# Gathered rows turned by transposing DMAs from ScalarE instead of TensorE transposes and a copy: a routed feed-forward kernel on one Trainium2 core

## The chip, the cores and the metric

The kernel runs on one core of a Trainium2 chip. The metric is device time in microseconds, the median of three runs.

## The reference, cut to what matters

For each of four batches of 1024 tokens by 1024 features, a 0/1 mask `m` of the same shape is made first (the 10,240 largest entries of `softmax(x) * side * cond`, without the diagonal). The mask's rows are then the input of a mixture of eight experts, two chosen for each row, and the result is added to `x`:

```python
scores = softmax(m @ G); value, indices = top_k(scores, 2)
w      = one_hot(indices, 8) weighted with value          # [b, s, e]
gate   = silu(einsum('bsh,efh->bsef', m, gate_w))
up     = einsum('bsh,efh->bsef', m, up_w)                 # F = 128
out    = einsum('bsef,bse,ehf->bsh', gate * up, w, down_w)
lr     = einsum('bsh,erh->bser', m, lora_A)               # R = 16
out    = out + einsum('bser,bse,ehr->bsh', lr, w, lora_B)
result = x + out
```

## The kernel before, in words

All weights are cut into f16 parts and held in SBUF for the whole run. Each batch is worked off in `T` = 23 tiles of up to 128 (row, expert) pairs, each tile for one expert. The work is written out by hand for each engine's queue; every queue runs in order, and engines wait for each other on semaphores. `tile(n, i)` = 23 n + i numbers the tiles through all batches.

For tile i of batch n, in the order of the data:

- GpSimd (`gather`, L514) fetches the tile's rows of the mask from `mask_rows` in HBM by an indirect DMA into `xg`, a ring of `NX` = 3 buffers of 128 rows by 1024 f16. It waits until the rows of three tiles back have been turned. GpSimd's loop over i issues `gather(i + 3)`, then `put_out(i - 3)`, then work for the next batch's mask, then `sum_piece` of the batch before.
- TensorE (`turn_x`, L668) transposes the tile's eight 128x128 blocks into one PSUM bank, and ScalarE (`store_xt`, L840) copies the bank to `xt`, two buffers of eight blocks. The copy waits until the first layer of two tiles back has read the buffer (`l1_done`).
- TensorE (`first_layer`, L681) multiplies: 16 matmuls with the blocks of `xt` as weights and `w1` moving, into `pa`.
- ScalarE (`silu`, L845) and VectorE (`gate`, L1342 to L1350) make the gated product; TensorE (`turn_g`, L692) transposes it, VectorE stores it, and TensorE (`second_layer`, L704 to L707) makes 2 x 4 matmuls of 512 columns into `pc`.
- ScalarE (`store_y`, L853) scales into `y`, and GpSimd (`put_out`, L522) scatters the rows to `put_rows` in HBM by an indirect DMA.

TensorE's queue for step i is: `first_layer(i)`, `turn_x(i + 2)`, `turn_g(i - 1)`, `second_layer(i - 2)`, with pieces of the next batch's work between them. ScalarE's is: `silu(i)`, `store_xt(i + 2)`, both halves of `store_y(i - 2)`, with counts of the next batch's mask (tiles 3 to 6, 8 and 9) and copies of its transposed mask (tiles 18 to 22) between them. A batch starts with `turn_x` of tiles 0 and 1.

Beside this, the results of the batch before are put together in 16 pieces of 128x512 (one per step in steps 1 to 9 and 13 to 19), in two buffers `piece`: SyncE loads x and the two scattered rows of each token (L367, L369), GpSimd adds them (L531, L534), SyncE stores the sum (L376) and only then loads the next piece into that buffer. Near the end of batches 0 to 2 SyncE (`move_mask`) loads the x of the batch after next, or for the last time the x of the last batch, and stores the finished mask to `mask_rows`. After the last batch SyncE loads the scattered rows, VectorE adds (L1449) and SyncE stores.

Of the kernel before, what the change touches and what calls it, by code (L numbers as in the profile page):

```python
# [6 lines left out]
ACT = mybir.ActivationFunctionType  # L7
AX = mybir.AxisListType
F32 = mybir.dt.float32
F16 = mybir.dt.float16  # L10
BF16 = mybir.dt.bfloat16
I32 = mybir.dt.int32
U32 = mybir.dt.uint32

P = 128
# [18 lines left out]
def build(nc, x, side, cond, G, gate_w, up_w, down_w, lora_A, lora_B, out):  # L34
# [70 lines left out]
    with ExitStack() as ctx:  # L105
# [6 lines left out]
        def sem(name):  # L112
            return ctx.enter_context(nc.semaphore(name))
# [121 lines left out]
        def table_of(n, i, dt=F32):  # L235
# [17 lines left out]
        l1 = [pa[:, i, 0:N1] for i in range(2)]  # L253
        xt_ps = blocks(pb[:, 0, :])
        gt_ps = blocks(pb[:, 1, :])[:, 0:3, :]
        mt_ps = blocks(pd[:, :])

        xt_words, gt_words, mt_words = pb[:, 0, :], pb[:, 1, 0:3 * P // 2].bitcast(I32), pd[:, :]
        words_of = lambda a, dt: a.rearrange("p t k -> p (t k)").bitcast(dt)
# [44 lines left out]
        last_summed, last_stored = sem("last_summed"), sem("last_stored")  # L304
        xt_turned, xt_ready, l1_done, silu_done = (
            sem(n) for n in ("xt_turned", "xt_ready", "l1_done", "silu_done"))
        g_ready, gt_turned, gt_ready, y_done, y_ready = (
# [14 lines left out]
        def tile(n, i):  # L322
            return T * n + i
# [4 lines left out]
        def _(sp):  # L328
# [50 lines left out]
            def move_mask(n):  # L379

                sp.wait_ge(mask_ready, n + 1)
                if n + 1 < B:
                    load_side(n + 1)
                    load_x(n + 1)
                else:
                    for c in range(C):
                        sp.dma_start(v[:, c, :], x_rows[n][:, c, :]).then_inc(last_x_landed[c], 16)
                if n >= 2:

                    sp.wait_ge(xt_turned, tile(n - 1, 0))  # L390
                sp.dma_start(mask_rows[n % 2].rearrange("(p c) h -> p (c h)", c=C),
                             mask[:, :]).then_inc(mask_stored, 16)
# [39 lines left out]
        def _(pool):  # L432
# [77 lines left out]
            def gather(n, i):  # L510
                g = tile(n, i)
                if g >= NX:
                    pool.wait_ge(xt_turned, g - NX + 1)
                pool.indirect_dma_start(  # L514
# [46 lines left out]
        def _(pe):  # L561
# [99 lines left out]

            def turn_x(n, i):
                g = tile(n, i)
                pe.wait_ge(gathered[g % NX], 16 * (g // NX + 1))
                if g > 0:
                    pe.wait_ge(xt_ready, g)
                for t in range(HT):
                    last = pe.transpose(xt_ps[:, t, :], xg[:, g % NX, t * P:(t + 1) * P], ident[:, :])  # L668
                last.then_inc(xt_turned, 1)

            def load_expert(n, i):
                return pe.value_load(expert[n][0:1, i:i + 1], min_val=0, max_val=E - 1)

            def first_layer(n, i, e):
                g = tile(n, i)
                pe.wait_ge(xt_ready, g + 1)
                if g >= 2:
# [56 lines left out]
            for n in range(B):  # L734
                pe.wait_ge(routed, n + 1)
                turn_x(n, 0)
                turn_x(n, 1)
                experts = {}
# [21 lines left out]
                for i in range(T):  # L760
                    experts[i] = load_expert(n, i)
                    first_layer(n, i, experts[i])
                    between(i, 0)
                    if i + 2 < T:
                        turn_x(n, i + 2)
                    between(i, 1)
# [17 lines left out]
        def _(act):  # L784
# [49 lines left out]

            def store_xt(n, i):
                g = tile(n, i)
                act.wait_ge(xt_turned, g + 1)
                if g >= 2:
                    act.wait_ge(l1_done, g - 1)
                nc.scalar.activation(words_of(xt[:, g % 2, :, :], F32), xt_words, ACT.Copy).then_inc(xt_ready, 1)  # L840

# [55 lines left out]
            for n in range(B):  # L897
# [8 lines left out]

                store_xt(n, 0)
                store_xt(n, 1)
                for i in range(T):
                    silu(n, i)  # L910
                    between(i, 0)
                    if i + 2 < T:
                        store_xt(n, i + 2)
                    between(i, 1)
# [565 lines left out]
```

## Time and profile before

| | |
|---|---|
| time, median of 3 runs | 810.81 us (809.69 to 813.43) |
| the profiled execution's own time | 809.9 us |
| its span, first to last instruction | 808.2 us |
| TensorE matmuls (PE), busy | 518.8 us (64%) |
| VectorE (DVE), busy | 515.5 us (64%) |
| ScalarE (ACT), busy | 403.3 us (50%) |
| GpSimd (POOL), busy | 391.1 us (48%) |
| mean granted clock of TensorE | 0.846 |

Times in the views count from the start of the span. PEld is the loading of weights, which runs beside the matmuls; SPq, POOLq and DVEq are an engine's own queue. Busy shares are means over stages with different limits: the first 160 us make the first mask and cut the weights, then come four batches of 23 tiles, and from about 770 us on the last batch's results are put together. Of an arrow `a<-b`, a is written and b read; buffer numbers are left out. An arrow behind a wait names what ended it.

### The profile page before, as it was taken

The page shows a single profiled execution, that of the slowest core. Times are in us where ns is not written, and L with a number is a line of the kernel's source. Part 1 is how long each engine was busy: PE and PEld are TensorE (multiplying, and loading weights), DVE is VectorE, ACT ScalarE, POOL GpSimd, SP SyncE. Part 2 cuts the span into 40 slices and gives each one's busy share as a digit, 9 for nine tenths or more (in the row PEclk, how much of TensorE's full clock was granted, in tenths as well). Part 3 has the DMA queues.
Part 4 walks back from the last instruction along what each step waited for, and adds up shares of the span by engine and source line. Part 5 has one row for each costly group of instructions (what it writes and reads, how often), then busy time and mean ns, then how long its engine had stood idle before and what let it go on. Part 6 is the DMA issues. An engine that isn't in the chain of part 4 may idle for free.

```text
span 808.2 us, 14610 instructions
## 1 busy us (share of the span) xinstructions
PE 518.8 (64%) x4178; PEld 356.4 (44%) x4178; DVE 515.5 (64%) x1242; ACT 403.3 (50%) x655; POOL 391.1 (48%) x337
## 2 busy tenths in 40 slices
PE   0211287179878964778787917787798288897900
PEld 0200276056645633455455515554556155565500
DVE  5768889766798575865884776747872623233335
ACT  5687277739734463376344453783344234354400
POOL 8114200125484114477886125878872167767510
PEclk9755599579999895899999868998989779899965
DMA  9990160024323734478377834685579258868469
GB/s 313 360 264 0 51 263 27 13 65 157 121 105 113 276 126 130 150 250 283 133 258 256 340 101 157 218 293 186 192 247 380 81 153 291 270 215 271 173 253 381
DMA packets 80443, 159.93 MB, mean 198 GB/s; under 512 B 22889, under 2 KB 32105, under 8 KB 79856
## 3 DMA queue, kind: packets, MB, share of 16 engines
q1 hardware_dynamic: 59760, 108.60, 39.4%
q0 software_dynamic: 20608, 50.37, 17.9%
q8 instruction: 43, 0.70, 0.4%
q14 instruction: 32, 0.26, 0.1%
HBM read 107.53 MB, written 73.40 MB: 224 GB/s over the span
## 4 chain that ended last, share of the span: by engine, by line
DMA 26%; POOL 18%; issue 16%; DVE 14%; PE 13%; ACT 6%; DVEq 3%; SPq 3%; POOLq 1%; ACTq 0%
DMA out_dram<-piece 7%; DMA piece<-put_rows 7%; DMA put_rows<-y,where 6%; POOL piece L531 4%; DMA xg<-mask_rows,where 4%; POOL piece L534 4%; PE pa L681 4%; POOL xg L514 3%; ACT mask L796 3%; POOL put_rows L522 3%; DVE w L1172 2%; DMA w<-put_rows 2%; DVE mask L1066 2%; PE pb L668 2%; ACT y L853 2%
## 5 line engine op out<-in xcount | busy, mean ns | idle before, releaser
L681 PE MATMUL pa<-w,xt 128*128 x1472 | 199.4, 289 | 1.2 <-issue 1.2
L853 ACT ACTIVATE y<-pc,where 128x512 f32<-128x512 f32 x184 | 124.5, 686 | 105.9 <-PE pc L707 82.2
L681 PEld LDWEIGHTS pa<-w,xt 128*128 128x128 f16 x1472 | 147.0, 100 | 56.6 <-issue 10.5
L514 POOL DMA_INDIRECT xg<-mask_rows,where x92 | 100.0, 1087 | 122.9 <-DVEq L1334 94.8
L522 POOL DMA_INDIRECT put_rows<-y,where x92 | 92.2, 1003 | 130.9 <-ACT y L853 109.8
L1342 DVE SCALAR_TENSOR_TENSOR g_full<-pa,where,s_act 128x144 f32<-128x144 f32 x92 | 33.6, 365 | 180.4 <-ACT s_act L845 180.0
L668 PE MATMUL pb<-ident,xg 128*128 128x128 f16 x736 | 62.8, 234 | 77.1 <-DMA xg<-mask_rows,where 58.1
L840 ACT ACTIVATE xt<-pb 128x512 f32<-128x512 f32 x92 | 55.0, 598 | 109.1 <-PE pb L668 105.5
L668 PEld LDWEIGHTS pb<-ident,xg 128*128 128x128 f16 x736 | 49.7, 105 | 87.7 <-DMA xg<-mask_rows,where 61.6
L845 ACT ACTIVATE s_act<-pa,small 128x128 f32<-128x128 f32 x92 | 33.8, 367 | 98.3 <-PE pa L681 98.3
L704 PE MATMUL pc<-wd,gt 128*128 x184 | 75.7, 411 | 5.4 <-ACT y L853 5.3
L705 PE MATMUL pc<-wd,gt 128*128 x184 | 75.3, 409 | 0.0
L531 POOL TENSOR_TENSOR piece<-piece 128x512 f32<-128x512 f32 x48 | 61.1, 1272 | 28.5 <-DMA piece<-put_rows 28.0
L706 PE MATMUL pc<-wd,gt 128*128 x184 | 74.7, 406 | 0.0
L707 PE MATMUL pc<-lb,gt 128*128 x184 | 74.4, 405 | 0.0
L796 ACT ACTIVATE mask<-v,small 128x1280 f16<-128x1280 f32 x48 | 65.0, 1355 | 8.2 <-POOL v L470 5.5
L534 POOL TENSOR_TENSOR piece<-piece 128x512 f32<-128x512 f32 x48 | 62.7, 1307 | 3.8
L1350 DVE TENSOR_TENSOR g_parts<-g_full,g_parts 128x144 f16<-128x144 f32 x92 | 44.7, 486 | 6.8
L937 DVE TENSOR_REDUCE small<-v 128x1 f32<-128x1024 f32 x32 | 38.4, 1214 | 14.9 <-DMA v<-in_x_dram 14.6
L1010 DVE TENSOR_SCALAR_CACHE_REDUCE mask<-v,small 128x1024 f16<-128x1024 f32 x36 | 44.9, 1273 | 2.8 <-POOL v L470 2.1
L957 DVE SCALAR_TENSOR_TENSOR v<-v,small,t_row 128x1024 f32<-128x1024 f32 x32 | 43.6, 1400 | 0.7
L692 PE MATMUL pb<-ident,g_parts 128*128 128x128 f16 x276 | 32.4, 229 | 15.0 <-DVE gt L1358 14.9
(208 smaller groups left out, 864.0 us busy)
## 6 DMA issues: line engine op xcount, KB each, us to landing
piece<-put_rows SPq DMA_DIRECT2D x96, 256.0 KB
v<-in_x_dram SPq DMA_DIRECT2D x40, 512.0 KB, 8.9
piece<-in_x_dram SPq DMA_DIRECT2D x48, 256.0 KB
out_dram<-piece SPq DMA_DIRECT2D x48, 256.0 KB
mask_rows<-mask SPq DMA_DIRECT2D x4, 2048.0 KB, 17.5
w<-put_rows SPq DMA_DIRECT2D x16, 512.0 KB, 9.9
w<-in_L_ffn_gate_w_dram SPq DMA_DIRECT2D x8, 512.0 KB, 10.2
w<-in_L_ffn_up_w_dram SPq DMA_DIRECT2D x8, 512.0 KB, 8.3
```

The source lines that it names most:

```text
L514: pool.indirect_dma_start(out=xg[:, g % NX, :], out_offset=None, in_=mask_rows[n % 2], in_offset=bass.IndirectOffsetOnAxis(ap=mask_row[n][ ...
L522: pool.indirect_dma_start(out=put_rows[n % 2], out_offset=bass.IndirectOffsetOnAxis(ap=put_row[n][:, i:i + 1], axis=0), in_=y[:, g % NY, : ...
L531: nc.gpsimd.tensor_tensor(piece[:, at, 0, :], piece[:, at, 0, :], piece[:, at, 1, :], ALU.add).then_inc(half_summed, 1)
L534: nc.gpsimd.tensor_tensor(piece[:, at, 0, :], piece[:, at, 0, :], piece[:, at, 2, :], ALU.add).then_inc(summed_piece, 1)
L668: last = pe.transpose(xt_ps[:, t, :], xg[:, g % NX, t * P:(t + 1) * P], ident[:, :])
L681: last = pe.matmul(l1[g % 2], xt[:, g % 2, t, :], w1[:, bass.ds(e, 1), t, k, :].rearrange("p o n -> p (o n)"), start=(t == 0 and k == 0), ...
L704: pe.matmul(pc[:, half, :], high, own(wd[:, bass.ds(e, 1), 0, cols]), start=True, stop=False)
L705: pe.matmul(pc[:, half, :], high, own(wd[:, bass.ds(e, 1), 1, cols]), start=False, stop=False)
L706: pe.matmul(pc[:, half, :], low, own(wd[:, bass.ds(e, 1), 0, cols]), start=False, stop=False)
L707: pe.matmul(pc[:, half, :], lora, own(lb[:, bass.ds(e, 1), cols]), start=False, stop=True).then_inc(y_done, 1)
L796: nc.scalar.activation(mask[:, cols], v_flat[:, cols], ACT.Sign, bias=t_at[k - 1], scale=-1.0, accum_out=act_cnt[:, p:p + 1]).then_inc(act ...
L853: nc.scalar.activation(y[:, g % NY, half * HALF:(half + 1) * HALF], pc[:, half, :], ACT.Copy, scale=y_scale[n][:, i:i + 1]).then_inc(y_rea ...
```

## The change

The TensorE transposes of the gathered rows and ScalarE's copy of them are replaced by one transposing DMA for each tile, issued from ScalarE's queue at the place of the copy: from `xg` (128 partitions by 1024 f16) into `xt` (eight blocks of 128x128). ScalarE waits for the gather and for `l1_done` of two tiles back before it issues. Each of the two `xt` buffers has its own semaphore `xt_landed`, and three places wait for it in place of `xt_turned` or `xt_ready`: the first layer, the gather that overwrites `xg` three tiles on, and SyncE's store of the mask in batches 1 to 3.

```diff
--- before.py
+++ after.py
@@ -251,11 +251,10 @@
         blocks_of = lambda b: b[:, :, :].rearrange("p a b -> p (a b)").bitcast(F16).rearrange(
             "p (e j k) -> p e j k", e=2, j=HT)
         l1 = [pa[:, i, 0:N1] for i in range(2)]
-        xt_ps = blocks(pb[:, 0, :])
         gt_ps = blocks(pb[:, 1, :])[:, 0:3, :]
         mt_ps = blocks(pd[:, :])
 
-        xt_words, gt_words, mt_words = pb[:, 0, :], pb[:, 1, 0:3 * P // 2].bitcast(I32), pd[:, :]
+        gt_words, mt_words = pb[:, 1, 0:3 * P // 2].bitcast(I32), pd[:, :]
         words_of = lambda a, dt: a.rearrange("p t k -> p (t k)").bitcast(dt)
         spread_ps = pd[:, 0:NEAR * P]
         lora_ps = [blocks_of(b) for b in (pa, pb, pc, pa)]
@@ -302,8 +301,8 @@
         last_x_landed = [sem(f"last_x_landed{c}") for c in range(C)]
         rows_landed = [sem(f"rows_landed{c}") for c in range(C)]
         last_summed, last_stored = sem("last_summed"), sem("last_stored")
-        xt_turned, xt_ready, l1_done, silu_done = (
-            sem(n) for n in ("xt_turned", "xt_ready", "l1_done", "silu_done"))
+        xt_landed = [sem(f"xt_landed{i}") for i in range(2)]
+        l1_done, silu_done = (sem(n) for n in ("l1_done", "silu_done"))
         g_ready, gt_turned, gt_ready, y_done, y_ready = (
             sem(n) for n in ("g_ready", "gt_turned", "gt_ready", "y_done", "y_ready"))
 
@@ -387,7 +386,8 @@
                         sp.dma_start(v[:, c, :], x_rows[n][:, c, :]).then_inc(last_x_landed[c], 16)
                 if n >= 2:
 
-                    sp.wait_ge(xt_turned, tile(n - 1, 0))
+                    for i in range(2):
+                        sp.wait_ge(xt_landed[i], 16 * len(range(i, tile(n - 1, 0), 2)))
                 sp.dma_start(mask_rows[n % 2].rearrange("(p c) h -> p (c h)", c=C),
                              mask[:, :]).then_inc(mask_stored, 16)
 
@@ -510,7 +510,7 @@
             def gather(n, i):
                 g = tile(n, i)
                 if g >= NX:
-                    pool.wait_ge(xt_turned, g - NX + 1)
+                    pool.wait_ge(xt_landed[(g - NX) % 2], 16 * ((g - NX) // 2 + 1))
                 pool.indirect_dma_start(
                     out=xg[:, g % NX, :], out_offset=None, in_=mask_rows[n % 2],
                     in_offset=bass.IndirectOffsetOnAxis(ap=mask_row[n][:, i:i + 1], axis=0),
@@ -659,21 +659,12 @@
                                      start=(q == 0), stop=(q == Q - 1))
                 last.then_inc(slots_ready, 1)
 
-            def turn_x(n, i):
-                g = tile(n, i)
-                pe.wait_ge(gathered[g % NX], 16 * (g // NX + 1))
-                if g > 0:
-                    pe.wait_ge(xt_ready, g)
-                for t in range(HT):
-                    last = pe.transpose(xt_ps[:, t, :], xg[:, g % NX, t * P:(t + 1) * P], ident[:, :])
-                last.then_inc(xt_turned, 1)
-
             def load_expert(n, i):
                 return pe.value_load(expert[n][0:1, i:i + 1], min_val=0, max_val=E - 1)
 
             def first_layer(n, i, e):
                 g = tile(n, i)
-                pe.wait_ge(xt_ready, g + 1)
+                pe.wait_ge(xt_landed[g % 2], 16 * (g // 2 + 1))
                 if g >= 2:
                     pe.wait_ge(g_ready, g - 1)
                 for t in range(HT):
@@ -733,8 +724,6 @@
 
             for n in range(B):
                 pe.wait_ge(routed, n + 1)
-                turn_x(n, 0)
-                turn_x(n, 1)
                 experts = {}
                 more = n + 1 < B
 
@@ -761,8 +750,6 @@
                     experts[i] = load_expert(n, i)
                     first_layer(n, i, experts[i])
                     between(i, 0)
-                    if i + 2 < T:
-                        turn_x(n, i + 2)
                     between(i, 1)
                     if i >= 1:
                         turn_g(n, i - 1)
@@ -832,12 +819,13 @@
                 act.wait_ge(mask_turned, C * n + c + 1)
                 nc.scalar.activation(words_of(mt[:, c % 2, :, :], F32), mt_words, ACT.Copy).then_inc(mt_ready, 1)
 
-            def store_xt(n, i):
+            def turn_rows(n, i):
                 g = tile(n, i)
-                act.wait_ge(xt_turned, g + 1)
+                act.wait_ge(gathered[g % NX], 16 * (g // NX + 1))
                 if g >= 2:
                     act.wait_ge(l1_done, g - 1)
-                nc.scalar.activation(words_of(xt[:, g % 2, :, :], F32), xt_words, ACT.Copy).then_inc(xt_ready, 1)
+                act.dma_start_transpose(out=xt[:, g % 2, :, :],
+                                        in_=xg[:, g % NX, :]).then_inc(xt_landed[g % 2], 16)
 
             def silu(n, i):
                 g = tile(n, i)
@@ -904,13 +892,13 @@
                     if more and (i, spot) in STORE_MT_AT:
                         store_mt(n + 1, STORE_MT_AT[i, spot])
 
-                store_xt(n, 0)
-                store_xt(n, 1)
+                turn_rows(n, 0)
+                turn_rows(n, 1)
                 for i in range(T):
                     silu(n, i)
                     between(i, 0)
                     if i + 2 < T:
-                        store_xt(n, i + 2)
+                        turn_rows(n, i + 2)
                     between(i, 1)
                     if i >= 2:
                         store_y(n, i - 2, 0)
```

## Rows read from the trace of the kernel before

**Rows 1.** Page, chain that ended last: share of the span by line.

```profile
DMA out_dram<-piece 7%; DMA piece<-put_rows 7%; DMA put_rows<-y,where 6%; POOL piece L531 4%; DMA xg<-mask_rows,where 4%; POOL piece L534 4%; PE pa L681 4%; POOL xg L514 3%; ACT mask L796 3%; POOL put_rows L522 3%; DVE w L1172 2%; DMA w<-put_rows 2%; DVE mask L1066 2%; PE pb L668 2%; ACT y L853 2%
```

**Rows 2.** Busy us by stage: PE, PEld, DVE, ACT, POOL; granted clock, DMA share, GB/s.

```profile
215.00:292.00 77.00, 65.30 (x566) 44.34 (x564) 58.00 (x121) 34.31 (x61) 33.25 (x27) 0.93 0.44 160
340.00:380.00 40.00, 33.07 (x253) 22.13 (x252) 25.36 (x77) 30.14 (x52) 30.95 (x28) 0.96 0.78 260
```

**Rows 3.** Chain in order of time, 349 to 362: start us, us, what.

```profile
349.67 4.57 DMA out_dram<-piece
354.25 0.33 SPq L367
...
355.18 4.19 DMA piece<-put_rows
...
359.45 1.26 POOL piece L531
360.79 1.27 POOL piece L534
```

**Rows 4.** Groups of instructions: count, busy us, mean ns, idle before, releasers.

```profile
L668 PE MATMUL pb<-ident,xg 128*128 128x128 f16 x736 | 62.8, 234 | 77.1 <-DMA xg<-mask_rows,where 58.1 <-issue 17.3 <-ACT xt L840 1.6
...
L840 ACT ACTIVATE xt<-pb 128x512 f32<-128x512 f32 x92 | 55.0, 598 | 109.1 <-PE pb L668 105.5
```

**Rows 5.** One line's instructions, batch 0: duration ns min/median/max, first and last start.

```profile
L681 PE MATMUL pa<-w,xt x368: 276/279/434, 164.9 to 287.8; 128*128 x184
```

**Rows 6.** Waits, longest first: us in total, times, longest us.

```profile
PE pb L668 <- DMA xg<-mask_rows,where: 58.1, 30, 6.5
...
POOL v L470 <- DVE v L957: 40.4, 4, 12.6
...
POOL piece L531 <- DMA piece<-put_rows: 28.0, 27, 2.5
...
POOL xg L514 <- PE pb L668: 10.5, 8, 2.7
```

**Rows 7.** Timeline, start of the third batch: start us, us, instruction, idle before.

```profile
484.24 1.01 PE L668 MATMUL pb<-ident,xg 128*128 128x128 f16 x8 [5.73 <-issue]
...
486.08 0.99 POOL L514 DMA_INDIRECT xg<-mask_rows,where  x1 [1.74 <-PE pb L668]
...
486.93 3.81 PE L681 MATMUL pa<-w,xt 128*128 x16
...
490.77 0.37 ACT L845 ACTIVATE s_act<-pa,small 128x128 f32<-128x128 f32 x1 [1.79 <-PE pa L681]
...
492.36 2.10 POOL L514 DMA_INDIRECT xg<-mask_rows,where  x1 [0.91 <-PE pb L668]
...
494.23 2.01 PE L681 MATMUL pa<-w,xt 128*128 x16
```

**Rows 8.** Timeline, around one late gather of the last batch.

```profile
686.07 0.86 PE L668 MATMUL pb<-ident,xg 128*128 128x128 f16 x8 [2.97 <-DMA xg<-mask_rows,where]
...
690.10 2.02 PE L681 MATMUL pa<-w,xt 128*128 x16
```

**Rows 9.** DMA queues (packets, MB, share) and issues (count, us to landing).

```profile
q1 hardware_dynamic: 59760, 108.60, 39.4%
...
xg<-mask_rows,where POOLq DMA_INDIRECT x92, 3.7
```

**Rows 10.** Chain by line in 170 to 292, 330 to 445, 665 to 765.

```profile
by line: issue 21.3%; DMA put_rows<-y,where 9.2%; ACT mask L796 7.2%; PE pa L681 6.8%; DMA xg<-mask_rows,where 5.6%; DVE mask L1066 5.1%; ACT y L853 5.0%; POOL mask L484 3.5%; PE pc L707 3.4%; PE pc L704 3.4%; PE pc L706 3.4%; PE pc L705 3.
...
by line: issue 20.6%; DMA out_dram<-piece 18.7%; DMA piece<-put_rows 14.6%; POOL piece L531 8.8%; POOL xg L514 6.8%; DMA xg<-mask_rows,where 6.7%; POOL piece L534 6.7%; POOL put_rows L522 6.3%; POOL mask L484 3.7%; POOL t_row L484 3.0%; SPq
...
by line: DMA piece<-put_rows 21.7%; DMA out_dram<-piece 19.4%; POOL piece L531 10.1%; POOL piece L534 8.7%; DMA xg<-mask_rows,where 8.6%; PE pa L681 5.9%; issue 5.7%; SPq L369 3.3%; POOL put_rows L522 3.0%; PE pc L704 2.2%; PE pc L705 2.2%;
```

**Rows 11.** Chain in order of time, ends of batches 0 and 1.

```profile
275.84 11.28 DMA put_rows<-y,where
...
435.72 7.76 DMA xg<-mask_rows,where
```

## The prediction

> **What bounds the kernel now.** I read the chain of waits first, then the busy time by stage, then the chain in order of time, the groups of instructions, the waits, and last two stretches of the timeline with the DMA issues. The page's chain gives no compute engine the lead: the stores and loads of `piece`, the row stores and the gathers come before any TensorE line, and the transposes that the change removes, `PE pb L668`, hold 2% of the span [rows 1]. 2% of 808.2 us is 16 us. That is the first thing to see: L668 is busy 62.8 us and its copy L840 55.0 us [rows 4], but most of that runs beside other work.
>
> The stages differ. In batch 0, where no pieces are summed yet, TensorE is busy 65.30 of 77 us and the DMA share is 0.44; its 23 first layers run from 164.9 to 287.8, 5.4 us per tile [rows 2, 5]. In the batches after, the DMA share is 0.78 and GpSimd is busy 30.95 of 40 us, beside 33.07 of TensorE [rows 2]. The chain in order of time shows why: store of a piece 4.57 us, SyncE's next issue, loads landing 4.19 us later, two sums on GpSimd of 1.26 and 1.27 us, then the next store of that buffer. From 349.67 to the end of the second sum at 362.06 is 12.4 us for one turn of one of two buffers, so 6.2 us per piece and per tile, 8.8 us of the turn being DMA [rows 3]. GpSimd waits for a piece's loads 27 times of 48, 28.0 us in all [rows 6]. So three of four batches are paced by a loop of transfers and GpSimd, not by TensorE.
>
> One more thing to see: TensorE takes its queue in order, so a late gather stops it at `turn_x`: 58.1 us in 30 waits [rows 6]. At 686.07 it had stood 2.97 us for a gather, and the next first layer, which does not need that gather, came only at 690.10 [rows 8].
>
> **The change, part by part.**
>
> *Batch starts.* Nothing overlaps the first tile. In the third batch the gather's rows are there at 484.24; behind two tiles' transposes and a copy the first layer starts at 486.93 [rows 7]. After the change ScalarE issues a DMA at 484.24 instead. The trace of before has no transposing DMA. The nearest row for its landing is the gather's median of 3.7 us, for the same 256 KB [rows 9]; the far one is a row store's 11.28 us in a burst [rows 11]. I take 4.0 us, the gather and a little for ScalarE's issue (0.33 us on SyncE in rows 3, 0.99 us on GpSimd in rows 7). The first layer then starts at 488.2, 1.3 us later. The third tile's transpose may only be issued when the first layer of tile 0 (3.8 us) and its silu (0.4 us) are done: 488.2 + 3.8 + 0.4 + 4.0 = 496.4, where that first layer now starts at 494.23 [rows 7]. GpSimd's gather for the tile three further on waits for that landing, and the sum of a piece is queued behind it; SyncE's store of that piece waits for the sum. In batches 0 to 2 GpSimd then stands anyway for VectorE's scaled rows (40.4 us in 4 waits, rows 6), which covers this; in the last batch nothing does, and a gather like that of 492.36 goes out at 496.4, 4.0 us late. Starts: 3 x 1.3 + 4.0 = +8 us. A landing of 2.7 us would make it about 0, one of 11.28 us above +40.
>
> *TensorE's transposes and the copy go away* (736 transposes, 92 copies). Worth only what is on the chain: 16 us, less about 2 us at each of the four starts, which the first term has already (the two groups of 1.01 us in rows 7): -8 us. The copy's 0.6 us on ScalarE is replaced by an issue of 0.33 to 0.99 us, so ScalarE comes out even to slightly worse; the upper end would cost 0.4 us in each of the six tiles of a batch in which ScalarE also counts for the next batch, 7 us over three batches, which I leave to the range.
>
> *The wait for the gather moves from TensorE to ScalarE.* Queued behind it on ScalarE are `store_y` of two tiles back and the next silu; before, ScalarE waited at the same place, behind the transposes. TensorE is now free to run the second layer and the next first layer during a late gather. The gathers hold 5.6% of the chain in 170 to 292, 6.7% in 330 to 445 and 8.6% in 665 to 765 [rows 10]: 6.8 + 7.7 + 8.6 = 23 us. All of it would be the bound; I take half, -12 us, because the loop of pieces and GpSimd is close behind in two of the three stretches.
>
> *92 transfers of 256 KB more on the 16 DMA engines.* Price of one, as time of all 16 engines: below, a plain transfer on the hardware queue: 39.4% of 808.2 us is 318 us for 108.60 MB, 2.93 us per MB, 0.77 us for one; above, if it goes in runs of one 128-column block (128 partitions x 8 runs of 256 bytes) and each costs what a packet costs on that queue (318 us x 16 / 59,760 = 85 ns), 1,024 x 85 ns / 16 = 5.4 us [rows 9]. I take 1.0 us, near the lower end, because the bytes are the same and only the runs are shorter. In the piece stretches a turn of the loop is 8.8 / 12.4 = 71% DMA and sees two transposes: 2 x 0.71 x 1.0 = 1.4 us per turn, 0.7 us per piece. It counts where GpSimd waits for the loads, 27 of 48: 0.4 x 48 = +19 us. At 0.77 us it would be +15, at nothing (all inside slack) 0, at 5.4 us over 100.
>
> *The bursts at the ends of batches 0, 1 and 2.* There the mask's rows are stored and the next x is loaded; a row store took 11.28 us and a gather 7.76 us [rows 11]. A transpose issued then queues as these did. With two `xt` buffers, tile i+2 can start its first layer one first layer (2.02 us in rows 8), 0.4 us to the end of the silu and one landing after tile i started, so the period is (2.4 + landing) / 2: 5.1 us at a landing of 7.76, 6.8 us at 11.28, against 5.4 us now. Four tiles per burst, three bursts: 0 to +17 us; between the two, +9 us.
>
> Also moved: GpSimd's gather waits for the landing of the tile three back instead of its transposes. It now meets that wait only 8 times, 10.5 us in all [rows 6], since it mostly comes later than the transposes end; a landing of 4 us is covered by the tile that lies between, one of 8 us is not. SyncE's wait before a mask store is on transposes of a batch ago, free.
>
> Sum: +8 - 8 - 12 + 19 + 9 = +16 us on the profiled execution's 809.9 us (1.7 us of it outside the span): 826 us. That execution is 0.9 us under the median of the runs shown, 810.81, which changes nothing here.
>
> **Rivals.**
>
> *Faster: the transfers hide.* If the added DMA time falls into slack everywhere (no contention term, landings in the bursts like the gather's), what is left is +8 - 8 and up to -23: 787 to 798 us, say 795. For it: GpSimd waits only 28.0 us for pieces in all, and TensorE is the engine nearest to its limit in batch 0. Against it: a DMA share of 0.78 with a loop that is two thirds DMA. It decides if one transpose costs less than about 0.3 us of that loop per tile.
>
> *Much slower: the landing closes the loop of two `xt` buffers.* Period (2.4 + landing) / 2. It exceeds 5.4 us from a landing of 8.4 us on, and the 6.2 us of a piece tile from 10.0 us on. The longest landing of this size in the trace is 11.28 us, in a burst [rows 11]. At that length everywhere the period is 6.8 us: 48 piece tiles x 0.6 + 44 others x 1.4 = +90 us in place of the burst term: 809.9 + 8 - 8 - 12 + 19 + 90 = 907 us; at 10 us it is 6.2, +35, 852 us. Between them, 880 us. It also covers the case that the transfer is carried out in pieces far smaller than 256 bytes, so that it is no single transfer in effect.
> The trace shows the eight TensorE transposes of a tile done in 0.86 and 1.01 us [rows 7, 8]. The Trainium skill, page "VectorE: DVE Perf Modes", section "The three transpose paths", puts one 128x128 block at 1309 ns through the DMA's crossbar against 390 ns on TensorE, and its rules advise TensorE where a PSUM destination is acceptable, so it speaks against this change. Eight blocks one after another would, by an estimate from that page, be 10.5 us per tile, and the time then lies inside this rival's; no row of before shows a transposing DMA.
>
> *No measurable change.* The gains (-20) and the losses (+36) meet if contention and bursts cost half of what I take and the starts 4 us: 809.9 - 20 + 18 = 808 us. Nothing but the size of the terms speaks for or against.
>
> **How the numbers follow.** My sum 0.42 (its own range 814 to 850), faster 0.29, loop closed 0.16, no change 0.13. Half a per cent, 4 us, is about what a measurement of this kernel can tell. Slower: 0.42 + 0.16 = 0.58; same 0.13; faster 0.29. The range from 788 to 892 us reaches into both side cases and leaves out about 2 in 10: the full gain with no contention below, a landing of some 11 us everywhere above.
>
> **What the profile after would show.** L668 and L840 gone, TensorE's busy time down by 63 us and ScalarE's by up to 55. A row for the `xt` transfers with a landing near 4 us, and near 8 to 11 us in the bursts. The wait of 58.1 us for gathers gone from TensorE and replaced by a wait of the first layer for `xt`, longest at the four starts. Turns of the piece loop near 13 to 14 us instead of 12.4, and more than 28.0 us of GpSimd waiting for pieces. If those turns stay at 12 us, the faster rival holds; if the first layers of every stage wait for `xt` and the period is that landing plus 2.4 us, halved, the slow one. ScalarE standing over 1 us at each issue, or a granted clock of TensorE below its present mean with its matmuls longer, would be something I left out.

## The result, and the profile after

The changed kernel takes 925.08 us (median of 4 runs, 915.52 to 932.73) against 812.12 us for the kernel before on the same chip: a ratio of 1.1336, 95% interval 1.1272 to 1.1401. One of these four runs, 932.73 us, and the profiled one of the idle transposes below, 890.39 us, fall in a slower state that the ratios leave out: by the ratio the change costs some 108 us, by the medians, which the sums below use, 113 us. The prediction was 826 us with a range up to 892 us. The direction was right, the size was not, and the range did not hold it. The profiled execution took 927.28 us, its span 925.6 us.

The page of the changed kernel: its DMA queues (packets, MB, share of 16 engines) and the chain that ended last, by engine and by line.

```profile
q1 hardware_dynamic: 59760, 108.60, 38.7%
q10 hardware_dynamic: 97152, 24.13, 18.1%
...
DMA 40%; DVE 15%; POOL 12%; issue 11%; PE 10%; DVEq 4%; ACT 4%; SPq 3%; ACTq 1%; POOLq 1%
DMA xt<-xg 13%; DMA out_dram<-piece 11%; DMA piece<-put_rows 8%; DMA xg<-mask_rows,where 6%; PE pa L672 5%; POOL piece L531 3%; POOL piece L534 2%; ACT mask L783 2%; POOL xg L514 2%; DVE w L1160 2%; DVE mask L1054 2%; DMA w<-put_rows 2%; DVE small L1016 2%; SPq L368 2%; POOL put_rows L522 1%
```

Queue q10 is new: it carries the 92 transposing DMAs, 97,152 / 92 = 1,056 packets each. They take 18.1% of 925.6 us, so 1.82 us of all 16 engines per transfer. In the chain the transfer `xt<-xg` now leads with 13%, before the stores of pieces, which rose from 7% to 11% [rows 1].

Waits of the changed kernel, longest first (us in total, times, longest), then its ScalarE instructions that write `xt`, and the first layers of the changed kernel and of the kernel before. A landing is the time from a DMA's issue until its data are there.

```profile
ACT y L841 <- DMA put_rows<-y,where: 179.9, 37, 15.0
...
PE pa L672 <- DMA xt<-xg: 149.6, 35, 18.6
...
POOL piece L531 <- DMA piece<-put_rows: 92.1, 30, 8.9
...
POOL xg L514 <- DMA xt<-xg: 40.0, 11, 7.1
```

```profile
L827 ACTq DMA_TRANSPOSE xt<-xg x92: 1247/1253/8865, 161.3 to 874.6; - x92
```

```profile
L672 PE MATMUL pa<-w,xt 128*128 x1472 | 228.5, 315 | 153.5 <-DMA xt<-xg 149.6 <-issue 3.4
```

```profile
L681 PE MATMUL pa<-w,xt 128*128 x1472 | 199.4, 289 | 1.2 <-issue 1.2
```

TensorE's 58.1 us of waiting for gathers has become 149.6 us for `xt`, GpSimd waits 92.1 us for pieces in place of 28.0 us [rows 6], and ScalarE's queue is held 1.25 us by each usual issue, once 8.87 us. The longest wait of all, 179.9 us of ScalarE for the row stores that free `y`, is not the loss by itself: the kernel without turning, below, has 161.4 us of it and is no slower than the kernel before.

Busy us by stage (PE, PEld, DVE, ACT, POOL; granted clock, DMA share, GB/s), the stretches of [rows 2].

```profile
215.00:292.00 77.00, 53.59 (x380) 33.11 (x378) 53.41 (x113) 24.46 (x44) 33.19 (x27) 0.91 0.70 205
340.00:380.00 40.00, 29.25 (x170) 17.25 (x170) 27.76 (x68) 19.08 (x33) 24.63 (x20) 0.89 0.93 228
```

The second stretch is the one to look at. The DMA engines are busy 0.93 of the time in place of 0.78, and they move less: 228 GB/s in place of 260 [rows 2].

Chain in order of time, one turn of the loop of pieces, the counterpart of [rows 3].

```profile
372.31 5.67 DMA out_dram<-piece
...
378.00 0.33 SPq L366
...
378.85 6.85 DMA piece<-put_rows
...
385.77 1.27 POOL piece L531
...
387.12 1.28 POOL piece L534
```

From the store's start to the end of the second sum it is 16.1 us, against 12.4 us in [rows 3], and all of the difference is in the two transfers.

Timeline at the end of batch 0 and in batch 1: SyncE's and ScalarE's issues and first layers, with what ended the idle time before.

```profile
268.67 4.37 SPq L330 DMA_DIRECT2D v<-in_x_dram  x8
...
273.08 0.45 SPq L391 DMA_DIRECT2D mask_rows<-mask  x1
...
273.78 1.49 ACTq L827 DMA_TRANSPOSE xt<-xg  x1
...
279.21 8.87 ACTq L827 DMA_TRANSPOSE xt<-xg  x1
...
291.46 0.89 PE L672 MATMUL pa<-w,xt 128*128 x3 [9.62 <-DMA xt<-xg]
...
484.07 3.41 PE L672 MATMUL pa<-w,xt 128*128 x16 [9.97 <-DMA xt<-xg]
510.76 1.54 PE L672 MATMUL pa<-w,xt 128*128 x6 [18.55 <-DMA xt<-xg]
```

The transfer issued at 273.78, right behind the loads of the next x and the store of the mask, lets the first layer start only at 291.46. Batch 1 has two such places. Before the second one the chain holds the gather of that tile and then its transfer, the longest of all:

```profile
467.93 15.76 DMA xg<-mask_rows,where
483.71 26.92 DMA xt<-xg
```

Where the time is lost, batch by batch: us from the first layer of tile 0 to that of the next batch (in batch 3 to the end of the span), from the trace of each kernel. The lower four kernels are experiments, told below.

| kernel | batch 0 | batch 1 | batch 2 | batch 3 |
|---|---|---|---|---|
| before | 153.0 | 169.0 | 165.5 | 155.8 |
| after | 167.9 | 210.5 | 202.5 | 178.9 |
| plain copies, 2 KB packets | 151.7 | 171.7 | 173.3 | 160.8 |
| plain copies, 256-byte packets | 163.5 | 186.1 | 186.3 | 164.9 |
| before, no pieces | 151.6 | 160.2 | 159.0 | 143.7 |
| after, no pieces | 169.0 | 176.4 | 175.8 | 143.3 |

In batch 0 of the changed kernel, where no pieces are moved yet, the first layer of tile 20 starts 110.5 us after that of tile 0, where it was 109.9 us before. So nothing is lost before the burst, and nothing is gained by the TensorE work that went.

### The profile page after: what moved, and what is told of

Its sections match the earlier page's. It is cut to its first block, busy times and chain, and to the rows that moved or that the text cites. A ratio compares the mean times of both kernels' runs of the same rounds, so it can differ in the third digit from the quotient of the medians.

```text
span 925.6 us, 13049 instructions
## 1 busy us (share of the span) xinstructions
PE 510.2 (55%) x3442; PEld 322.9 (35%) x3442; DVE 509.4 (55%) x1242; ACT 344.7 (37%) x563; POOL 387.7 (42%) x337
## 3 DMA queue, kind: packets, MB, share of 16 engines
q10 hardware_dynamic: 97152, 24.13, 18.1%
q0 software_dynamic: 20608, 50.37, 17.4%
## 4 chain that ended last, share of the span: by engine, by line
DMA 40%; DVE 15%; POOL 12%; issue 11%; PE 10%; DVEq 4%; ACT 4%; SPq 3%; ACTq 1%; POOLq 1%
DMA xt<-xg 13%; DMA out_dram<-piece 11%; DMA piece<-put_rows 8%; DMA xg<-mask_rows,where 6%; PE pa L672 5%; POOL piece L531 3%; POOL piece L534 2%; ACT mask L783 2%; POOL xg L514 2%; DVE w L1160 2%; DVE mask L1054 2%; DMA w<-put_rows 2%; DVE small L1016 2%; SPq L368 2%; POOL put_rows L522 1%
## 5 line engine op out<-in xcount | busy, mean ns | idle before, releaser
L672 PE MATMUL pa<-w,xt 128*128 x1472 | 228.5, 315 | 153.5 <-DMA xt<-xg 149.6
L672 PEld LDWEIGHTS pa<-w,xt 128*128 128x128 f16 x1472 | 156.6, 107 | 237.9 <-issue 182.8
L841 ACT ACTIVATE y<-pc,where 128x512 f32<-128x512 f32 x184 | 120.5, 683 | 278.6 <-DMA put_rows<-y,where 179.9
L531 POOL TENSOR_TENSOR piece<-piece 128x512 f32<-128x512 f32 x48 | 61.0, 1271 | 92.5 <-DMA piece<-put_rows 92.1
L534 POOL TENSOR_TENSOR piece<-piece 128x512 f32<-128x512 f32 x48 | 60.7, 1265 | 3.8
L998 DVE TENSOR_SCALAR_CACHE_REDUCE mask<-v,small 128x1024 f16<-128x1024 f32 x36 | 45.0, 1273 | 2.5 <-POOL v L470 1.7
L1338 DVE TENSOR_TENSOR g_parts<-g_full,g_parts 128x144 f16<-128x144 f32 x92 | 42.3, 459 | 6.8
L945 DVE SCALAR_TENSOR_TENSOR v<-v,small,t_row 128x1024 f32<-128x1024 f32 x32 | 39.7, 1279 | 0.6
L1054 DVE TENSOR_SCALAR_CACHE_REDUCE mask<-v,small 128x1024 f16<-128x1024 f32 x32 | 39.2, 1275 | 0.5
L774 ACT ACTIVATE v<-v,small 128x1024 f32<-128x1024 f32 x32 | 36.4, 1141 | 7.2 <-DVE small L925 7.0
L484 POOL TENSOR_TENSOR t_row<-v,mask 128x1024 f32<-128x1024 f32 x12 | 25.6, 2131 | 30.3 <-PE pm L576 21.5
## 6 DMA issues: line engine op xcount, KB each, us to landing
w<-in_L_ffn_gate_w_dram SPq DMA_DIRECT2D x8, 512.0 KB, 10.2
```

The source lines that it names most:

```text
L531: nc.gpsimd.tensor_tensor(piece[:, at, 0, :], piece[:, at, 0, :], piece[:, at, 1, :], ALU.add).then_inc(half_summed, 1)
L534: nc.gpsimd.tensor_tensor(piece[:, at, 0, :], piece[:, at, 0, :], piece[:, at, 2, :], ALU.add).then_inc(summed_piece, 1)
L672: last = pe.matmul(l1[g % 2], xt[:, g % 2, t, :], w1[:, bass.ds(e, 1), t, k, :].rearrange("p o n -> p (o n)"), start=(t == 0 and k == 0), ...
L841: nc.scalar.activation(y[:, g % NY, half * HALF:(half + 1) * HALF], pc[:, half, :], ACT.Copy, scale=y_scale[n][:, i:i + 1]).then_inc(y_rea ...
L1054: V.tensor_scalar(mask[:, c * S:(c + 1) * S], v[:, c, :], now, None, ALU.is_ge, ALU.add, accum_out=row_count[:, c:c + 1])
```

## The experiments

Three groups: what the transfers cost when nobody waits for them, what is paid for waiting, and what there was to gain.

### Idle transfers beside the kernel before

**Idle transposes.** The room is that of the LoRA weights, so the fourth product of the second layer reads other weights.

```diff
 def store_xt(n, i):
     ...
+    act.dma_start_transpose(out=lb[:, g % 2, :].rearrange("p (t k) -> p t k", t=HT),
+                            in_=wd[:, g % E, 0, :]).then_inc(idle_landed[g % 2], 16)
```

> The kernel before, with 92 idle transposing DMAs beside its own path: behind each copy to xt, ScalarE also issues a transposing DMA of 256 KB from weights that rest in SBUF into the room of the LoRA weights, and nobody uses the result (ScalarE only keeps two in flight). So that this room is free, the fourth product of the second layer reads other weights: its result is another. Theory A (the transfers themselves cost: 1,056 packets each, 1.8 us of all 16 DMA engines, and issues that ScalarE must sit out in the bursts): piece turns and bursts get slower as in the changed kernel, 870 us or more, of which at least 30 us in the bodies of batches 1 to 3. Theory B (the cost is that the first layer and the next gather wait for a landing, the traffic itself is hidden): 812 to 822 us.

Measured: 875.33 us (890.39 us in the profiled run), against 812.06 us: +63 us, with no engine waiting for their data.

**Idle plain copies** of the same bytes, `act.dma_start(lb[:, g % 2, :], wd[:, g % E, 0, :])`, 144 packets each.

> As the run with idle transposes, but the 92 idle DMAs are plain copies of the same 256 KB, in rows of 2,048 bytes (the fourth product of the second layer again reads other weights). Theory A with the small packets as its cause: 815 to 830 us, far below the idle transposes. Theory A with the bytes as its cause: within 15 us of the idle transposes. Theory B: 812 to 822 us, as the idle transposes.

Measured: 833.23 us, ratio 1.0281 (1.0144 to 1.0417). That is 3 us above what I expected if small packets were the cause. The bytes are a part, some 21 us, but not the main one.

**Idle plain copies in 256-byte packets.**

```diff
+    act.dma_start(lb[:, g % 2, :].rearrange("p (t k) -> p t k", t=HT),
+                  wd[:, :, 0, 0:P]).then_inc(idle_landed[g % 2], 16)
```

> The kernel before (TensorE still turns the rows), with one idle plain copy of 256 KB per tile issued by ScalarE where the idle transposes stood, cut into runs of 256 bytes (1,024 per copy), read from the second layer's weights and written to room that nothing reads; the fourth product of the second layer reads other weights instead of that room. If the number of 256-byte packets is the cost (theory), it comes near the idle transposes: 860 to 890 us. If the transposing itself or ScalarE's longer issue is the cost (rival), it comes near the idle copies in runs of 2 KB: 825 to 845 us.

Measured: 826.11 us, ratio 1.0184 (1.0094 to 1.0275). My theory fell: the count of packets is not what makes the idle transposes dear either. The idle transfers' queue in the two kernels, first the transposes, then these copies.

```profile
q10 hardware_dynamic: 97152, 24.13, 20.9%
```

```profile
q10 hardware_dynamic: 95680, 24.12, 13.0%
```

The packets are all but equally many, and yet the transposes hold the engines for 2.02 us each (20.9% of 888.6 us, over 92) and the copies for 1.17 us (13.0% of 825.4 us). The stretch 345 to 445, mostly the body of batch 1, shows what that does to the others. In order: before, the idle small copies, the idle transposes, after.

```profile
345.00:445.00 100.00, 78.76 (x632) 52.60 (x631) 66.96 (x160) 51.06 (x90) 78.46 (x64) 0.96 0.72 239
```

```profile
345.00:445.00 100.00, 77.69 (x624) 52.52 (x623) 66.27 (x157) 49.55 (x85) 77.13 (x64) 0.95 0.86 270
```

```profile
345.00:445.00 100.00, 75.89 (x515) 46.56 (x514) 65.10 (x151) 47.55 (x82) 67.32 (x54) 0.89 0.94 228
```

```profile
345.00:445.00 100.00, 74.87 (x403) 42.71 (x404) 61.80 (x148) 39.06 (x67) 67.75 (x55) 0.83 0.94 235
```

Read the last two columns. Small plain packets raise the share to 0.86 and the rate to 270 GB/s: they are added to the rest. Transposes raise the share to 0.94 and lower the rate to 228: they push the rest aside. From the records of single packets, adding up what other queues start between the first and the last packet of each added transfer: some 196 GB/s while a small copy is in flight and 194 otherwise; 135 to 146 and 203 to 207 for idle transposes, 130 to 141 and 188 to 193 in the changed kernel, by how transfers that overlap are told apart. Batch 3, which has no burst, takes 178.6 us beside idle transposes and 162.6 us beside the small copies.

**Is it ScalarE's longer issue?** The small copies hold ScalarE's queue 0.60 us each, transposes 1.25 us, so an idle activation of about 0.6 us was put beside each small copy.

```diff
+    nc.scalar.activation(lb[:, 2, :].bitcast(F32), words_of(wd[:, 0, 0, :]...), ACT.Copy).then_inc(held, 1)
```

> The kernel before with the idle plain copies in runs of 256 bytes (826 us), and beside each an idle activation of 128x512 on ScalarE, about 0.6 us: ScalarE is then held by about 1.25 us per tile, as by the issue of a transposing DMA. It leaves out the fourth product's own weights. If ScalarE's hold is what makes idle transposes cost 56 us more than these copies (rival): 860 to 885 us. If it is the transposing transfer that shuts other transfers out (theory): 822 to 840 us.

Measured: 830.11 us, ratio 1.0243 (1.0164 to 1.0322). The usual hold is worth some 4 us, a difference that lies within the two intervals. This does not answer for the long holds in bursts: one idle transpose held the queue 12.42 us at the end of batch 0, and that batch took 165.6 us against 154.1 us with small copies. So of what idle transposes cost more than small copies, the hold can have a part in the bursts, and has little outside them.

### What is paid for waiting

**Plain copies in place of the transposes**, waited for in the same way; the rows are not turned.

```diff
-    act.dma_start_transpose(out=xt[:, g % 2, :, :],
-                            in_=xg[:, g % NX, :]).then_inc(xt_landed[g % 2], 16)
+    act.dma_start(xt[:, g % 2, :, :].rearrange("p t k -> p (t k)"),
+                  xg[:, g % NX, :]).then_inc(xt_landed[g % 2], 16)
```

> The changed kernel with plain copies in place of the transposing DMAs, same place, same waits, same bytes, in rows of 2,048 bytes; the rows reach the first layer unturned, so the result is another. Theory A (small packets): 800 to 835 us, since the landing falls back to that of a gather. Theory B (any DMA on this path costs its landing): 890 us or more.

Measured: 830.75 us, ratio 1.025 (1.006 to 1.044). A transfer in the path as such costs some 19 us, about what idle copies of this kind cost.

**The same in 256-byte packets**, `in_=xg[:, g % NX, 0:P].unsqueeze(1).to_broadcast([P, HT, P])`.

> The changed kernel with a plain copy in runs of 256 bytes (1,024 per tile, each block of a tile read from the first 128 columns of its gathered rows) in place of the transposing DMA, in the same place and waited for in the same way; the rows are not turned. If in the bursts it is the number of small packets beside the next batch's x that makes the first layers late, and in the rest of the batches the transposing (theory): the bursts cost as in the changed kernel, some 40 to 60 us, the rest as with plain copies, in all 850 to 885 us. If the transposing is behind both (rival): 825 to 840 us, as idle copies of this kind. If the packets are behind both: above 900 us.

Measured: 865.61 us against 813.23, ratio 1.0629 (1.0557 to 1.0702), as the theory had it. By the table, batches 0 to 2 lose 11.8, 14.4 and 13.0 us against the 2 KB copies and batch 3, which has no burst, 4.1 us. The end of batch 0 shows the same wait as in the changed kernel. Chain in order of time, 256-byte copies:

```profile
272.74 18.42 DMA xt<-xg
```

and the first layer of tile 21 with 2 KB copies, with the idle time before it:

```profile
279.83 2.35 PE L672 MATMUL pa<-w,xt 128*128 x16 [0.84 <-DMA xt<-xg]
```

18.42 us in the chain here, 17.54 us for the transfer of 273.78 in the changed kernel, and 0.84 us of waiting with large packets. In the bursts it is the small packets, transposing or not, queued beside packets of 4 and 16 KB. By the packets' records the copy of this tile took 12.1 us from first to last packet, of which it used the engines some 1.2 us; the 2 KB copy of that tile took 4.15 us.

Set side by side, the same place with the same waits costs 19 us with 2 KB copies, 52 us with 256-byte copies and 113 us with transposes: some 34 us for the small packets, most of it in the bursts, and some 61 us for the transposing.

**Bursts turned by TensorE.** Tiles 19 to 22 of batches 0 to 2 as before, all others by DMA.

```diff
+    def on_pe(g):
+        n, i = g // T, g % T
+        return n < B - 1 and i >= 19
```

> The changed kernel, but tiles 19 to 22 of batches 0 to 2, which meet the mask's store and the loads of x, are turned by TensorE and copied as before. If the bursts hold about 60 of the 113 us: 860 to 875 us, with the spans from the first to the last first layer of batches 0 to 2 shorter by 11, 30 and 17 us. If the loss there only moves on to the next wait: above 900 us.

Measured: 884.36 us, ratio 1.0912 (1.0812 to 1.1012). 41 us come back, 9 us less than the nearer end of the forecast: the bursts are a part, and the smaller one.

**DMA only in the first 19 tiles of batch 0**, `return n > 0 or i >= 19`.

> The changed kernel with the transposing DMA in the first 19 tiles of batch 0 alone, where no pieces are moved; every other tile is turned by TensorE and ScalarE as before. If the 113 us come from sharing the DMA engines with pieces and from the bursts (theory): 808 to 816 us, as before. If a transposing DMA costs in every tile whatever runs beside it (rival: 19 of 92 tiles at 113/92 us each, and more for ScalarE's hold at issue): 825 to 840 us.

Measured: 815.62 us, ratio 1.0045 (1.0005 to 1.0085): without pieces beside it and outside a burst a transposing DMA costs nearly nothing (some 3 us for 19), and gains nothing.

**Without pieces**, before and after: the loads and stores of batches 0 to 2 are left out in both.

```diff
-    sp.dma_start(piece[:, at, 0, :], x_rows[n][:, c, cols]).then_inc(piece_landed[at], 16)
-    for r in range(ROLES): ...
...
-    sp.dma_start(out_rows[n][:, c, half * HALF:(half + 1) * HALF], ...)
```

> The kernel before with the loads and stores of pieces of batches 0 to 2 left out (144 loads, 48 stores); GpSimd still makes the sums, on stale data. The base for the next kernel: 770 to 800 us, by tiles of 5.3 to 5.5 us in place of some 6 in batches 1 to 3.

> The changed kernel with the same left out. If a transposing DMA costs by sharing the engines with pieces (theory), the difference to the kernel before without pieces is that of the bursts and starts alone, 35 to 65 us, in place of 113. If it costs in itself (rival): 90 us or more.

Measured: 782.15 us and 832.07 us. The change costs 49.9 us here in place of 113.0, and by the table that is 17.4, 16.2 and 16.8 us in the batches with a burst and -0.4 us in batch 3. So 63 us of the loss go with the pieces, and the bursts, with the starts, make 50. The burst of batch 0 in the kernel without pieces, by the chain and by ScalarE's queue:

```profile
272.69 20.44 DMA xt<-xg
```

```profile
277.76 12.51 ACTq L821 DMA_TRANSPOSE xt<-xg  x1
```

**Deeper buffers.** Four buffers `xt`, five `xg`, issue three tiles ahead (`NX, NY, NXT = 5, 2, 4`; `turn_rows(n, i + 3)`), the room again from the LoRA weights.

> The changed kernel with four buffers of turned rows in place of two and five of gathered rows in place of three, the room taken from the fourth product's weights (which then reads others), and each transposing DMA issued three tiles ahead instead of two. The transfers are the same 92. If the 43 us between the idle transposes and the changed kernel are waits for landings (theory): 870 to 890 us. If it is traffic again, which more buffers don't lessen (rival): 910 to 930 us. If depth hides nearly all: below 850 us.

Measured: 873.67 us, ratio 1.0772 (1.0681 to 1.0863): 51 us back, down to the idle transposes' level. By the traces batches 1 and 2 are 33 and 16 us shorter than in the changed kernel, batch 3 some 5 us, but batch 0, which has only its burst, 1.8 us. The first layer's waits in this kernel:

```profile
PE pa L677 <- DMA lb<-xg: 19.4, 3, 10.1
...
PE pa L677 <- DMA lb<-lb: 12.7, 1, 12.7
PE pa L677 <- DMA xt<-xg: 11.6, 2, 11.2
```

With the fourth kind, 10.2 us, they come to 54 us in place of 149.6. Depth hides much of what waiting costs, though not in the burst of batch 0; what is left is about what the transfers cost when nobody waits for them.

### What there was to gain

**No turning at all** from the third tile on; the first layer waits for the gathered rows and reads the first two tiles' turned rows.

```diff
 def gather(n, i):
-    pool.wait_ge(xt_turned, g - NX + 1)
+    pool.wait_ge(l1_done, g - NX + 1)
 def turn_x(n, i):
+    if g >= 2: return
 def first_layer(n, i, e):
-    pe.wait_ge(xt_ready, g + 1)
+    pe.wait_ge(gathered[g % NX], 16 * (g // NX + 1))
+    pe.wait_ge(xt_ready, min(g + 1, 2))
```

> The kernel before without any turning from the third tile on: no TensorE transposes, no copy, no transfer in their place; the first layer waits for the gathered rows themselves and reads the first two tiles' turned rows again. It leaves out part of the computation. This is the most that the change could gain, with a transfer of no time and no cost. By the terms of the prediction (-8 for the work, -12 for the late gathers, and the starts, about 2 us each in three batches): 782 to 792 us. By the rival (what was removed lay beside VectorE, ScalarE and the loop of pieces): 802 to 812 us.

Measured: 807.31 us, ratio 0.9936 (0.9901 to 0.9971). It gains 5 us. Waits of this kernel, then the first of them in the kernel before:

```profile
ACT y L858 <- DMA put_rows<-y,where: 161.4, 50, 7.1
...
POOL xg L514 <- PE pa L684: 57.8, 21, 9.0
...
PE pa L684 <- DMA xg<-mask_rows,where: 17.4, 3, 5.8
```

```profile
ACT y L853 <- DMA put_rows<-y,where: 23.7, 12, 4.3
```

TensorE's waits for gathers fell from 58.1 us [rows 6] to 17.4 us at the first layer, but ScalarE now waits 161.4 us for the row stores that must free its two `y` buffers, and GpSimd 57.8 us for first layers. The rows go round by gather, layers and store; as I read these waits, a turn of that ring is hardly shorter for less TensorE work.

The 57.8 us say that 5 us is no proven upper bound. With no copy of the rows in `xt`, a gather must wait until the first layer of three tiles back has read `xg`, where it waited for transposes two steps earlier, so this kernel has fewer rows in flight. By its trace batches 0 and 1 are some 4.5 us shorter each than before, batches 2 and 3 2.4 and 7.1 us longer. Two places without that fault point the same way: where a transposing DMA costs next to nothing, in the first 19 tiles of batch 0 and in batch 3 without pieces, taking the work off TensorE gained nothing and 0.4 us.

**Transposes behind the second layer** in TensorE's queue, the copy behind `store_y`, so that a late gather stops only its own tile.

```diff
     if i >= 2:
         second_layer(n, i - 2, experts[i - 2])
     between(i, 3)
+    if i + 2 < T:
+        turn_x(n, i + 2)
```

> The kernel before with the transposes of a tile put behind the second layer on TensorE, and the copy behind the output copies on ScalarE, so that a late gather holds up only the first layer that needs it. If late gathers on TensorE cost what the prediction took (-12 us): 797 to 805 us. If a late gather's wait only takes the place of another (rival): 808 to 818 us, above the kernel before if the copy now comes too late for the first layer.

Measured: 809.27 us, ratio 0.997 (0.9924 to 1.0017), not told apart from the kernel before. Its waits, the gather's on TensorE and the row store's on ScalarE:

```profile
ACT y L853 <- DMA put_rows<-y,where: 113.9, 42, 5.6
...
PE pb L668 <- DMA xg<-mask_rows,where: 20.7, 13, 6.7
```

58.1 us became 20.7, while the waits for row stores rose from 23.7 to 113.9 us. No version of the change beat the kernel before.

## Why the prediction was wrong, step by step

**What bounds the kernel.** Right: the loop of pieces, DMA and GpSimd paces batches 1 to 3, and 63 of the 113 us go with that loop.

**Batch starts, +8.** Small, as said. The gaps from the last tile's first layer to the next batch's were 32.21, 33.60 and 34.49 us and are 35.20, 33.52 and 33.94 us; the first start of all is 1.0 us later. Together +3.4 us.

**TensorE's work gone, -8, and the gather's wait off TensorE, -12.** Wrong together: without any turning 5 us came back, in a kernel that has fewer rows in flight, and with the transposes only moved nothing that can be told apart. I read the gathers' share of the chain as gain and took half. With those waits gone, the waits for the row stores that free `y` grew by 138 us (161.4 against the 23.7 us of before).

**92 transfers, +19: the step that failed.** I took 1.0 us of the engines, "near the lower end, because the bytes are the same and only the runs are shorter". The runs were indeed 256 bytes, but the copies in such runs, at 1.17 us and +14 us, show that this price was fair for a plain transfer. The transposing one held the engines 1.82 us and pushed the others aside. Against the 256-byte copies in the same place that is some 61 us, and the loss without pieces is smaller by 63 us. The price alone does not make it: with 1.82 us my own formula gives 1.82 x 0.71 x 27 = +35 us. The discount "where GpSimd waits for the loads, 27 of 48" was wrong as well, since I took those waits as they were and they grew, from 28.0 us in 27 waits [rows 6] to 92.1 us in 30, and the turn shown went from 12.4 to 16.1 us. The upper bound, over 100 us, covered it; the choice between the bounds did not.

The Trainium skill, page "Advanced Engine Details and Errata", section "X-Bar Transpose (TRN2)", says that transposing DMAs are as fast as regular ones. By the packets' records the quickest tenth of the idle transposes took up to 1.4 us from first to last packet, of the 256-byte copies 1.3 us, which agrees, but of the copies in 2 KB packets 0.8 us, which does not. Beside the pieces the measurement decides: 875 us and more with idle transposes, 826 and 833 us with idle copies.

**Bursts, +9 (0 to +17): the second that failed.** I let a landing be at most the 11.28 us of [rows 11], a row store in packets of 4 KB. The small packets took 17.54 us in the chain at the end of batch 0 and 26.92 us in batch 1, where two late first layers stood 9.97 and 18.55 us, and a gather took 15.76 us where I had 7.76. Measured without pieces: some 17 us for each burst, 50 us in all.

**ScalarE's issue.** I took 0.33 to 0.99 us; it is 1.25 us, and up to 8.87 us in a burst. The first is worth some 4 us, within the noise. The second falls into the same time as the late landing, and the 256-byte copies, which held ScalarE 0.60 us there, lost 10.5 us in batch 0 against the kernel before, the transposes 14.9 us.

**The rivals.** "Faster" is out. "The landing closes the loop of two `xt` buffers" named a mechanism that is there, but had it at every tile: it acts above all on one or two transfers in each burst, and four buffers took 51 us back. Its time, up to 907 us, was too low as well, because the contention term beside it was. Its estimate from the page "VectorE: DVE Perf Modes" of the Trainium skill, section "The three transpose paths", 10.5 us per tile, is not what the traces show: the first transfer in batch 0 holds 4.43 us of the chain, a usual one in flight takes 1.4 to 2.7 us.

**What the profile would show.** L668 and L840 are gone, but TensorE's busy time fell by 8.6 us, not 63: a first-layer matmul's mean went from 289 to 315 ns, at a mean granted clock of 0.811 in place of 0.846. What the lower clock costs by itself was not separated.

What stays open: why a transposing transfer pushes others aside beside pieces. That it does is shown; no run here looks inside. The plain copies also leave each row in its partition, where a transpose carries data across all of them; no plain copy across partitions was run, so "transposing" here means both.

## What to carry to other kernels

Before moving work from an engine to a DMA, ask which loop of transfers paces that stage, and price the new transfer by its packets and by what it does to the others' GB/s, not by its bytes. Small packets are cheap until something waits for them beside a burst of large ones. And measure first what leaving the work out altogether would gain: here it was 5 us, and though that kernel is no exact bound, it would have warned me.

## What the hardware showed that I had not expected

A transposing DMA of 128x1024 f16 goes out as 1,056 packets and holds the issuing queue 1.25 us; a plain copy of the same bytes took 144 packets and 0.47 us. In a burst, behind a transpose still in flight, the next issue stood for 8.87 us in the changed kernel and 12.51 us without pieces; with four buffers `xt` no issue stood longer than 3.07 us.

A late landing also met a slower TensorE. Two stretches of the changed kernel, the second half of the 9.62 us of waiting before 291.46 and the first layer behind it (columns as above):

```profile
286.00:291.40 5.40, 0.00 (x0) 0.00 (x0) 0.00 (x0) 1.75 (x3) 0.98 (x1) 0.50 1.06 370
291.40:295.30 3.90, 3.84 (x18) 2.60 (x19) 0.00 (x0) 0.00 (x0) 0.00 (x0) 0.50 0.21 63
```

The granted clock is 0.50, the lower of the two levels, 1.2 GHz, and that first layer takes 3.84 us; the one of 276.40, at a granted clock of 1.00, took 2.27 us. So this late landing is paid a second time by the matmuls behind it.
